# Rank products behind the inverse transform, a first stage in groups of four orders, one body in the last stage's loops

## The reference

```python
coeff = complex(x[..., 0], x[..., 1]) * sqrt_eig
s = einsum('nlm,mlk->nkm', coeff, pct)              # per order m: sum over l
h = irfft(s, n=512, norm='forward')                 # (64, 256, 512)
# attention in a band of 12 rows, on xn = layernorm(h)
logits = tanh(xn @ K @ xn.T + bias) - 10000 * (1 - band)
h = h + softmax(logits * temperature) @ xn
# on x_bd = layernorm(h): a row counts if x_bd[0] >= 0.5 and x_bd[1] >= 0.5
# its nibbles (argmax over four fields of 16) go through 7 layers of 160;
# twice the one-hot of each rounded result is added to 32 columns
h = h + ffn(layernorm(h))
```

## Time and profile before

| what | value |
|---|---|
| median of three executions | 1552.46 us (1550.82 to 1553.61) |
| the profiled execution | 1550.52 us, its span 1548.7 us |
| stage 1 | 0 to 346.5 us of the span |
| stage 2 | 346.5 to about 1338.5 us |
| stage 3 | to the end |
| busy over the span | PE 88%, DVE 70%, ACT 43%, POOL 40% |
| DMA | 210.57 MB |

### The profile page before, as it was taken

One profiled execution on the slowest core, in us unless ns is written; L12 is line 12 of the kernel. 1 busy time (PEld: TensorE's weight loads), 2 busy tenths in 40 slices (PEclk: granted clock), 3 DMA queues, 4 the chain that ended last, 5 costly groups with the idle time before them and its releaser, 6 DMA issues. The chain is left out here.

```text
span 1548.7 us, 31360 instructions
## 1 busy us (share of the span) xinstructions
PE 1365.0 (88%) x9261; PEld 1191.6 (77%) x9261; DVE 1083.5 (70%) x2565; ACT 669.4 (43%) x1373; POOL 617.1 (40%) x1598
## 2 busy tenths in 40 slices
PE   4778777857999999999999999999999997399993
PEld 3666666747999999999999999999999986255551
DVE  1322222216899999999999999999999996377772
ACT  1222222122454554554544544545455443277772
POOL 2000000001365566555655665556556655302332
PEclk9789999897999999999999999999999999599997
DMA  9999999972211222212111221122112101100000
GB/s 374 428 427 430 428 427 429 427 268 90 70 70 71 69 79 73 70 69 81 71 68 69 76 74 69 68 81 69 68 69 79 59 30 42 37 1 12 10 4 5
DMA packets 58747, 210.57 MB, mean 136 GB/s; under 512 B 9413, under 2 KB 12177, under 8 KB 46289
## 3 DMA queue, kind: packets, MB, share of 16 engines
q1 hardware_dynamic: 47360, 172.29, 28.5%
q10 hardware_dynamic: 5200, 33.62, 5.4%
q0 software_dynamic: 6144, 4.14, 1.0%
HBM read 138.73 MB, written 73.07 MB: 137 GB/s over the span
## 5 line engine op out<-in xcount | busy, mean ns | idle before, releaser
L188 PE MATMUL s1b<-pg,cg 128*128 128x256 f32 x1024 | 248.7, 405 | 88.5 <-DVE cg L139 78.3
L188 PEld LDWEIGHTS s1b<-pg,cg 128*128 128x128 f32 x1024 | 206.3, 204 | 130.5 <-ACT stage L216 36.8
L428 PE MATMUL ps_kx<-xThi,Khi 128*128 128x256 f32 x1024 | 283.7, 277 | 4.0 <-DVE xTlo L680 4.0
L429 PE MATMUL ps_kx<-xTlo,Khi 128*128 128x256 f32 x1024 | 283.4, 277 | 0.0
L430 PE MATMUL ps_kx<-xThi,Klo 128*128 128x256 f32 x1024 | 283.4, 277 | 0.0
L139 DVE TENSOR_TENSOR cg<-xg,se 128x2048 f32<-128x2048 f32 x32 | 73.3, 2292 | 233.4 <-DMA pg<-in_pct_dram 226.0
L587 ACT ACTIVATE o<-h,sh,sc 128x512 f32<-128x512 f32 x128 | 97.5, 809 | 286.6 <-POOL sh L821 286.6
L428 PEld LDWEIGHTS ps_kx<-xThi,Khi 128*128 128x128 f32 x1024 | 193.2, 189 | 4.6 <-DVE xTlo L680 4.6
L429 PEld LDWEIGHTS ps_kx<-xTlo,Khi 128*128 128x128 f32 x1024 | 192.9, 188 | 0.0
L430 PEld LDWEIGHTS ps_kx<-xThi,Klo 128*128 128x128 f32 x1024 | 192.9, 188 | 0.0
L216 ACT COPY stage<-s1b 128x512 f32<-128x512 f32 x128 | 65.7, 598 | 234.3 <-PE s1b L188 234.3
(11 more groups left out here) (139 smaller groups left out, 3151.8 us busy)
## 6 DMA issues: line engine op xcount, KB each, us to landing
pg<-in_pct_dram SPq DMA_DIRECT2D x32, 2048.0 KB, 27.6
xg<-in_xs_dram SPq DMA_DIRECT2D x32, 1024.0 KB, 22.8
spec<-stage ACTq DMA_DIRECT2D x64, 512.0 KB, 8.5
xt<-spec SPq DMA_DIRECT2D x64, 512.0 KB, 3.6
out_dram<-o SPq DMA_DIRECT2D x64, 512.0 KB, 2.8
recs<-rec POOLq DMA_DIRECT2D x16, 160.0 KB, 16.5
recs<-rec,idx POOLq DMA_INDIRECT x128, 2.3
Kf<-in_K_dram SPq DMA_DIRECT2D x1, 1024.0 KB, 23.3
```

Of the source, the lines that this page charges most:

```text
L188: last = nc.tensor.matmul(bank[(b % 2) * 4 + m // 2][:, m % 2, :], cg[:, b % 2, m * 2 + h, :], pg[:, b, m * 2 + h, :], start=(h == 0), sto ...
L428: nc.tensor.matmul(out_ap, whi, mhi, start=(j == 0), stop=False)
L429: nc.tensor.matmul(out_ap, whi, mlo, start=False, stop=False)
```

## The change

Stage 1: groups of 4 orders, a ring of 8 groups, four `cg` buffers; PE signals every two orders, ACT copies each as it comes and stores every second group; order 256 is loaded, scaled and multiplied first and put in row 0 of the first store. The record fill moves from POOL in stage 1 to SP in stage 2, behind the first four loads; the loads of the last stage's matrices follow it there; their splitting moves to the start of stage 3. Stage 2: PE's `rank` and ACT's copy of its result go behind the inverse transform's; POOL makes `nom` and the record copies first, then the second layer norm, then index, row numbers and the indirect stores. Stage 3: ACT, PE and POOL loop over 16 passes with one body; SP and DVE keep two. SP loads the first records before it reads `count`.

The diff, cut:

```diff
-GM = 8
+GM = 4
-RING1 = 4
+RING1 = 8
+SETS = 4
+PARTS = GM // 2
...
 # stage 1, SP
+            sp.dma_start(x_top[:, :, :], xs_in[:, GROUPS * GM * 2:, :]).then_inc(top_loaded, 16)
+            sp.dma_start(p_top[:, :, :], pct_in[:, GROUPS * GM * 2:, :]).then_inc(top_loaded, 16)
...
-                if b == 1:
-                    for dst, src in ((Kf[:, :, :], K_in), (Wf[:, :, :], Wm_in), (W1f[:, :, :], W1_in), *others):
+                if b == RING1 // 2:
+                    for dst, src in ((Kf[:, :, :], K_in), *others):
...
 # stage 1, DVE
-                wait(dve, summed, g - 1)
+                wait(dve, summed, (g - SETS + 1) * PARTS)
...
 # stage 1, PE
-                wait(pe, copied, (g - 1) * 4)
+                wait(pe, copied, (g - SETS + 1) * PARTS)
+                for part in range(PARTS):
+                    for m in (2 * part, 2 * part + 1):
+                        for h in range(2):
+                            last = nc.tensor.matmul(bank[(b % SETS) * PARTS + part][:, m % 2, :],
+                                                    cg[:, b % SETS, m * 2 + h, :], pg[:, b, m * 2 + h, :],
+                                                    start=(h == 0), stop=(h == 1))
+                    last.then_inc(summed, 1)
...
 # stage 1, ACT
+                if b % 2 == 1:
+                    act.wait_ge(copied, g * PARTS + PARTS)
+                    for c in range(2):
+                        act.dma_start(spec[:, bass.ds(g * GM + (c * NLAT - GM), 2 * GM), :],
+                                      stage[c * NB:(c + 1) * NB, half]).then_inc(stored[half], 16)
...
 # stage 1, POOL
-            for q in range(NB * NLAT // (P * 8)):
-                pool.dma_start(view[:, q], rec0[:, :, :]).then_inc(rec_stored, 16)
...
 # stage 2, SP
             for n in range(4):
                 load(n, n)
+            sp.wait_ge(const.rec_filled, 2)
+            empty = recs.rearrange("(p q r) w -> p q r w", p=P, r=8)
+            for q in range(NB * NLAT // (P * 8)):
+                sp.dma_start(empty[:, q], const.rec0[:, :, :]).then_inc(rec_emptied, 16)
+            for dst, src in ffn_consts:
+                sp.dma_start(dst, src).then_inc(ffn_loaded, 16)
...
 # stage 2, PE
                 if has(i):
                     keys(i, k)
-                if has(i - 3):
-                    rank(i - 3, (k + 1) % 4)
                 if has(i - 1):
                     probs_T(i - 1)
                 if has(i + 2):
                     inverse_dft(i + 2, (k + 2) % 4)
+                if has(i - 3):
+                    rank(i - 3, (k + 1) % 4)
                 if has(i + 1):
                     x_T(i + 1, (k + 1) % 4)
...
 # stage 2, ACT: the copy of ps_l into pos (L549 to L553) goes behind od (L568)
...
 # stage 2, POOL
-                    pool.wait_ge(dve_v4, n + 1)
-                    pool.wait_ge(act_pos, n + 1)
                     settled(pool)
                     nc.gpsimd.tensor_scalar(nom[:, :], mask3[:, r2, 0:2], -FAR, FAR, ALU.mult,
                                             ALU.add).then_inc(pool_idx, 1)
-                    pool.wait_ge(pool_idx, n * 3 + 1)
-                    nc.gpsimd.tensor_tensor(fidx[:, :], pos[:, r2, 0:2], nom[:, :], ALU.add).then_inc(pool_idx, 1)
-                    pool.wait_ge(pool_idx, n * 3 + 2)
+                    nc.gpsimd.tensor_copy(rec[:, r4, :, 0], rows[:, :]).then_inc(pool_rec, 1)
+                    pool.wait_ge(dve_v4, n + 1)
                     settled(pool)
-                    nc.gpsimd.tensor_copy(idx[:, r4, :], fidx[:, :]).then_inc(pool_idx, 1)
-                    nc.gpsimd.tensor_copy(rec[:, r4, :, 0], rows[:, :]).then_inc(pool_rec, 1)
...
                 if has(i - 2):
...
                     nc.gpsimd.tensor_tensor(sh2[:, r2, :], dcT[:, :, bass.ds(n, 1)].rearrange("p t o -> p (t o)"), off[:, :],
                                             ALU.subtract).then_inc(pool_sc2, 1)
+                if has(i - 3):
+                    n, r4, r2 = i - 3, (k + 1) % 4, (k + 1) % 2
+                    pool.wait_ge(act_pos, n + 1)
+                    pool.wait_ge(pool_idx, n * 3 + 1)
+                    nc.gpsimd.tensor_tensor(fidx[:, :], pos[:, r2, 0:2], nom[:, :], ALU.add).then_inc(pool_idx, 1)
+                    pool.wait_ge(pool_idx, n * 3 + 2)
+                    settled(pool)
+                    nc.gpsimd.tensor_copy(idx[:, r4, :], fidx[:, :]).then_inc(pool_idx, 1)
+                    if isinstance(n, int) and n == 0:
+                        pool.wait_ge(rec_emptied, 16 * (NB * NLAT // (P * 8)))
+                    pool.wait_ge(pool_rec, n * 4 + 4)
+                    pool.wait_ge(pool_idx, n * 3 + 3)
+                    settled(pool)
+                    nc.gpsimd.tensor_scalar(rows[:, :], rows[:, :], float(NLAT * 16), None, ALU.add)
+                    for t in range(TILES):
+                        nc.gpsimd.indirect_dma_start(
...
 # stage 3
-        def steps(eng, ahead, body):
+        def steps(eng, at_once, ahead, body, phases=1):
             count = eng.value_load(const.count_i[0:1, 0:1], min_val=0, max_val=NB * NLAT)
+            at_once()
             with eng.If(count > 0):
                 ahead()
-            with eng.Fori(0, STEPS, 2) as s0:
-                for u in range(2):
+            with eng.Fori(0, STEPS, phases) as s0:
+                for u in range(phases):
...
-            sp.wait_ge(start, 2)
-            steps(nc.sync, lambda: load(0, 0), body)
+            load(0, 0)
+            steps(nc.sync, lambda: None, lambda: sp.nop(), body, phases=2)
...
+            def split_weights():
+                dve.wait_ge(weight_hi, 2)
+                nc.vector.tensor_tensor(W1r[:, :, :], const.W1f[:, :, :], W1h[:, :, :].bitcast(F32),
+                                        ALU.subtract).then_inc(weight_lo, 1)
+                nc.vector.tensor_tensor(Wlo[:, :, :], const.Wf[:, :, :], Whi[:, :, :].bitcast(F32),
+                                        ALU.subtract).then_inc(weight_lo, 1)
...
+            def ahead():
+                features(0, 0)
+                split_weights()
+            steps(nc.vector, ahead, first, body, phases=2)
...
+            nc.scalar.copy(W1h[:, :, :], const.W1f[:, :, :]).then_inc(weight_hi, 1)
+            nc.scalar.copy(Whi[:, :, :], const.Wf[:, :, :]).then_inc(weight_hi, 1)
+            steps(nc.scalar, lambda: round_in(0), first, body)
...
+            def ahead():
+                features_T(0)
+                pe.wait_ge(weight_lo, 4)
+            steps(nc.tensor, ahead, first, body)
...
-            steps(nc.gpsimd, lambda: pool.nop(), body)
+            steps(nc.gpsimd, lambda: None, lambda: pool.nop(), body)
```

More of the change, by code:

```diff
@@ L197, in _ @@
                     multiply(g0 + b, b)
-            pe.wait_ge(scaled, GROUPS + 1)
-            pe.wait_ge(copied, (GROUPS - 1) * 4)
-            for h in range(2):
-                last = nc.tensor.matmul(bank[0][:, 0, :], cg[:, 0, h, :], pg[:, 0, h, :],
-                                        start=(h == 0), stop=(h == 1))
-            last.then_inc(summed, 1)
         @block.scalar
@@ L218, in copy_out @@
-                act.wait_ge(copied, g * 4 + 4)
-                for c in range(2):
-                    act.dma_start(spec[:, bass.ds(g * GM + c * NLAT, GM), :],
-                                  stage[c * NB:(c + 1) * NB, b % 2]).then_inc(stored[b % 2], 16)
+                half, at = (b // 2) % 2, (b % 2) * GM
+                act.wait_ge(summed, g * PARTS + 1)
+                if b % 2 == 0:
+                    if isinstance(g, int):
+                        wait(act, stored[half], 32 * (g // 4))
+                    else:
+                        act.wait_ge(stored[half], g * 8 - 16 * half)
@@ new lines, in copy_out @@
+                for j in range(PARTS):
+                    if j > 0:
+                        act.wait_ge(summed, g * PARTS + j + 1)
+                    if isinstance(g, int) and g == 0 and j == 0:
+                        nc.scalar.copy(const.dc[:, :], bank[0][0:NB, 0, :])
+                    nc.scalar.copy(stage[:, half, at + 2 * j:at + 2 * j + 2, :],
+                                   bank[(b % SETS) * PARTS + j][:, :, :]).then_inc(copied, 1)
+                    if isinstance(g, int) and g == 0 and j == 0:
+                        act.wait_ge(copied, 1)
+                        act.wait_ge(top_summed, 1)
+                        nc.scalar.copy(stage[0:NB, 0, 0, :], bank[7][0:NB, 1, :]).then_inc(top_kept, 1)
+                        act.wait_ge(top_kept, 1)
@@ L548, in slot @@
                                        ps_kx[b][:, :]).then_inc(act_keyhi, 1)
-                if has(i - 3):
-                    n = i - 3
-                    act.wait_ge(pe_rank, n + 1)
-                    wait(act, pool_idx, (n - 1) * 3)
-                    nc.scalar.copy(pos[:, (k + 1) % 2, :], ps_l[:, 0, 0:3]).then_inc(act_pos, 1)
                 if has(i - 1):
@@ L1143, in body @@
                 results_T(s)
-            steps(nc.tensor, first, body)
```

(4 more changed lines are left out.)

162 lines of the change are left out of this document (71 added, 91 removed).

## The result

The changed kernel takes 1610.45 us (median of 4 runs, 1609.56 to 1613.61) against 1552.79 on the same chip: a ratio of 1.0377, 95% interval 1.0359 to 1.0395. The profiled execution took 1609.56 us, with a span of 1607.8. The span grew by 59.1 us, from 1548.7: stage 1 gave 6.4 back, stage 2 took 65.1 more, stage 3 took 0.4 more.

A forecast was written before the change was run, and what follows sets the result against it. Took the kernel as bound by stage 1's DMA stream, then a 14.74 us ring through POOL's stores, second norm and tanh. Terms -8 + 59 + 1.5 - 2 + 1 = +51 us gave 1604 us; range 1566 to 1640.

The forecast's parts named there:

- Stage 1: First stage: moved fill and matrices, early order 256, more packets and a shorter tail sum to about -8 us.
- rival 3: Stage 1 loads: halved transfers starve the stream to 374 GB/s, 46 us on top, 1648 us; chance 0.03.
- Fill and matrices at no cost: Stage 2 start: record fill and last-stage matrices delay block 4's load, covered by over 45 us until due; cost 0.
- Rank products renamed, worth nothing: Stage 2, PE: its wait for the mask becomes one for the exponential; at most 0.1 us a slot moves.
- The new slot: Stage 2, slots 3 to 61: 15.75 us against 14.74, +1.0 us each, +59 us in all.
- the ring that the forecast had: Stage 2, new order: band, DVE up to `mv`, second norm, index, stores, next band; taken as 15.75 us.
- Slot 2 of the trace: Stage 2, slot before the first rank: POOL waits directly for `mv`; band to `sh` 11.59 us, used for the new ring.
- The old slot: Stage 2 before: mask, rank, index, stores, second norm, `sh`, `o`, tanh, band close on themselves in 14.74 us.
- Rival 1: Stage 2: the PE wait goes and no ring replaces it, faster, say 1535 us; chance 0.12.
- Rival 2: Stage 2: the same ring with stores held up by DVE, 16.3 us a slot, 1636 to 1645 us; chance 0.10.
- Tail of stage 2: Last three slots: stores end the chain and POOL idles for `mv` once more; +1.5 us, between 0 and 3.
- Stage 3: Last stage: earlier record load -2 us, loop branches in idle passes at the end +1 us.

The follow-up runs named there:

- rank_early: Changed kernel with PE's rank products and ACT's copy of the ranks back in their old places, POOL's new order kept: 1611.3 us, ratio 1.0371.
- stores_first: Changed kernel with POOL's index, row numbers and indirect stores back ahead of the second norm, rank products still late: 1612.31 us, ratio 1.0381.
- both_back: Changed kernel with rank products, ACT's `pos` copy and POOL's index and stores back in place; `nom` and record copies stay early: 1545.77 us, ratio 0.9949.
- after_one: Changed kernel without one of an order's two indirect stores (records of the second half not written): 1551.0 us, ratio 0.9963.
- before_one: Kernel before the change without one of an order's two indirect stores (records of the second half not written): 1557.18 us, ratio 0.9996.
- th_first: both_back with ACT's output copy `o` behind the next slot's tanh instead of ahead of it: 1547.15 us, ratio 0.9932.
- xnlo_early: both_back with DVE's `xnlo` moved ahead of the first norm's statistics: 1578.23 us, ratio 1.0135.
- half_stats: both_back with DVE's first norm statistics over 128 of the 512 columns only: 1523.3 us, ratio 0.9774.
- xnlo_mid: both_back with DVE's `xnlo` behind `pTlo`, beside POOL's stores, and the second norm's aggregation right behind its statistics: 1575.26 us, ratio 1.0139.
- xnlo_th: both_back with the edits of both xnlo_early and th_first: 1540.66 us, ratio 0.9919.
- mid_poolfill: xnlo_mid with the record fill's sixteen transfers issued by POOL at the start of stage 2, not by SP: 1573.05 us.

## Why the prediction was right, and where not

1604 was forecast and 1610.45 measured, inside the range; the sum against the span was +51 (51.5 before rounding), and it is +59.1.

- **Stage 1**, -8: -6.4. The terms shifted among themselves. The bytes' 9.1 us were eaten: against the packets' 5 us, 260 us at 422 in place of 428 GB/s are 3.6, the last 27.5 us before the last scaling ran at 399 in place of 427 GB/s (1.8), the first 40 us moved 0.5 MB less (1.2). That is 6.6 us where 5 stood, and the last scaling came no earlier instead of 3.2 us earlier, so 1.6 more stay open. The tail gave 6.3 where I had 4.75.
- **The page's rule on DMA sizes.** The stream of 0.5 and 1 MB loads runs at 422 GB/s; the Trainium skill (DMA: Bandwidth & Descriptors, section Bandwidth) has 341 GB/s for 1 MB, measured there on transfers that GpSimd issues; these come from SP. The trace disagrees here too, and rival 3 is out.
- **Fill and matrices at no cost:** slot 2 is as long as before (14.17 and 14.18 us), but the way to the first band is 0.8 us longer; what does that was not tried. Slot 3 took 17.8 us (14.82 before), some 2 more than the new slot; 1.5 of them are the first store's later start and longer run. Taking POOL's plain DMAs away ahead of its first indirect store was a step that I did not have.
- **Rank products renamed, worth nothing:** right beside POOL's new order, by rank_early. By themselves they would have cost 1.0 us a slot (stores_first against both_back), through `pos`; the forecast did not ask that.
- **The new slot**, 15.75 us for 59 slots, +59 us: 15.77, and 62.2 us more for the 59 slots, 3.0 of them in slot 3. It is closed by the ring that the forecast had (band, DVE to `mv`, second norm, index, stores); after_one shows that the stores are on it. POOL's wait, 4.15 us a slot, was forecast as some 4.5; PE's, 1.3 us a slot, as about 1. Slot 2 of the trace was a good model, with the stretched `rstd` (1.00 and 1.02 us).
- **The old slot**: this step failed. It was "closed on itself" through the stores in my reading; before_one shows that it was not; th_first, xnlo_early and half_stats show what did close it. Without the 0.08 us for which the band was held (1.37 against 1.29), the store ring was at 14.67 us and DVE with the band at 14.75: two limits 0.1 us apart, and a ring drawn through instructions that follow one another closes for either. The forecast stood because it took the old spacing from the trace and worked out the new ring alone. Its side remark, that PE was 0.3 us short of being the bound, is not borne out: PE kept up with slots of 14.32 us, so it was at least 0.43 short.
- **Rival 1** (faster) would have needed the wait for `mv` to be short. **Rival 2** (a held store) did not occur, by luck of order: the first store starts before `xnlo`. xnlo_mid shows the mechanism, 0.94 us for one store; over 59 slots of a ring without slack that would be about 55 us more, an estimate.
- **Tail of stage 2**, +1.5: +2.1 behind slot 61. **Stage 3**, -1: +0.4. The start gave the 2.0 us forecast, although the split is not wholly covered (PE waits 1.30 us for DVE's `W` before the first layer), the end took 2.3 where +1 stood, inside its bound of 3; which of the loop's parts does it was not tried.

The Trainium skill (SBUF — State Buffer, section Who interferes with whom) has the rule behind the old slot: the pair of ports that VectorE and GpSimd share is a lock, whoever starts first keeps it for the whole instruction, and issue order decides who blocks. The traces agree in both directions (`band` 1.29 to 2.28 us behind `xnlo`, two `x` 0.58 to 1.37 behind the band). I had used it for `rstd` alone and never asked what the largest such pair in the slot was.

The fastest of these kernels that computes everything is xnlo_th: 1540.66 us, 0.9919 of the kernel before. Its slot is that of both_back (0.9949), and the two intervals touch, so the 0.3% between them is not shown to be real; about half of the gain is the first stage's 6.4 us.

## What to carry to other kernels

When a step is moved behind a late input, what stood in that wait's shadow comes after it: draw the new ring, and add it up from durations in the trace. To say what closes a ring today, look for an instruction whose duration gives way (1.37, 1.71, 1.72, 2.28 us for the same band): that is a place to test for the bound, though no wait is shown there. And two instructions of different engines that exclude each other are one resource: in the three moves of `xnlo` tried here, moving it only changed what was held.

## What was unexpected of the hardware

- An instruction held by the other engine's is not shown as idle but as longer: one `band` took 1.29 to 2.28 us, DVE read as busy 197 of 200 us with the work of 185.
- The same section of the Trainium skill infers that writing descriptors is not blocked by a VectorE instruction with two SBUF inputs. A store that started 0.15 us behind `xnlo` took 2.06 us in place of 1.12; one that had started 0.4 us before it took 1.12. Which part of the store is held was not tried.
- POOL's first indirect store comes later when no plain DMA of its own went before: the gap ahead of it was 0.61 to 0.64 us with such DMAs (before, before_one, mid_poolfill) and 1.49 to 4.70 in the eleven kernels without. What sets it between these two stays open.
